# Last stage of an attention and feed-forward kernel: inverse norms from a logarithm, an exponential and a Newton step per half tile, applied one tile later, with the rotation joined in place in six buffers

## The chip, the core and the metric

The kernel runs on one core of a Trainium2 chip. The metric is the device time of one execution in microseconds (us). The time before is the median of three runs.

## The reference

The program is a stack of four parts on `x` of shape (2, 512, 128): a cross attention, a mixture of attention experts, a second cross attention, and a six-layer local-attention transformer. The change lies in the last part alone, called stage D here. Cut to what matters, each of its six layers computes

```
x = attn_layer(shift_tokens(x), Wqkv[i], q_scale[i], k_scale[i], Wo[i]) + x
x = ffn_layer(shift_tokens(x), ln_g[i], ln_b[i], W1[i], b1[i], W2[i], b2[i]) + x

attn_layer:
  q, k, v = split(x @ Wqkv)                  # 16 heads of 64
  q = q / max(norm(q), 1e-12) * q_scale      # norm per token and head
  k = k / max(norm(k), 1e-12) * k_scale
  q = q * cos * scale + rotate_half(q) * sin * scale
  k = k * cos / scale + rotate_half(k) * sin / scale
  softmax over a window of 32 + 32 keys, times v, times Wo
```

The inverse norm is one number per token and head, so it commutes with the rotation: the kernel rotates the unnormalised q and k and multiplies by the inverse norm afterwards.

## The kernel before, in words

Stage D (`stage_d`) starts at about 1220 us of a 2410 us span. The 1024 tokens are 8 tiles of 128 (four per batch element). A layer's projection of a tile is cut in four chunks of 512 columns: chunks 0 and 1 are q, 2 and 3 are k, each of 8 heads. Chunk number `k = 4n + c` is chunk c of tile n.

One chunk passes through five engines. TensorE (PE) multiplies (L1256) into the PSUM bank `PM[:, 0]`; ScalarE (ACT) copies it to `RAW` (L1414) and squares it to `SQ` (L1423); VectorE (DVE) multiplies `RAW` by the tables into `R1` and, halves swapped, into `R2` (L1492 to L1494), sums the squares per head (L1496) and floors the sum (L1498); GpSimd (POOL) adds `R1 + R2` into `QR` (L1211), raises the eight floored sums to the power -0.5 (L1213) and multiplies `QR` by them (L1216). One tile later PE turns (transposes) the four 128-column blocks of `QR` into `PX` (L144, called from `proj`), and ACT copies them to `QT` or `KT` (L1419). Behind the turn, in the same chunk, PE makes v (L1269) in bank `PM[:, 1]`.

PE's part of a chunk is written so: first matmul L1256 of chunk k, then

```
wait(roped, k - 4)
wait(turned_out, k - 5)
for i in range(4):
    mm = turn(m, pe, PX[:, i * 128:(i + 1) * 128], QR[:, k % 4, i * 128:(i + 1) * 128])
```

and then the v matmuls. `roped` is what POOL's multiplication L1216 counts. Every engine runs its instructions strictly in its own order.

That order comes from a list written out by hand, `layer_order()`: for each step k of 0 to 12 it names pieces with a number, and each engine carries out what it has to do for a piece. Steps 9 to 12 of a layer are interleaved with steps 0 to 3 of the next (`BODY`, sorted by step and number), so one pass of the loop has steps 0 to 8. In step k, PE does: `score` of tile k-2 (L1281), `pturn` of tile k-3 (probabilities turned), `proj` chunk 0, chunk 1, `mix` (probabilities times v, L1302), chunk 2, `oturn`, chunk 3, and `out` (L1322). DVE does, in this order: the score's mask, maximum and subtraction (L1503, L1506, L1508), chunk 0, chunk 1, the weighting of the mixed values (L1519), chunk 2, the sum of the probabilities (L1511), chunk 3, and the addition of `out` (L1523). The feed-forward part has pieces `f1a`, `f1b`, `f2`, `f3`, `f4`. For one batch element they fall in steps 7 and 8, for the other in steps 2 and 3. In `f1b`, between chunks 1 and 2 (behind `mix`), DVE takes the variance (L1529 to L1537), POOL raises it to -0.5 (L1220) and DVE scales (L1540). In `f3`, ACT's Gelu (L1453) needs a table load, and so does the next Exp (L1431).

`R1`, `R2`, `RAW` and `SQ` have two buffers each, `QR` four. DVE therefore waits for `roped` of chunk k-2 before it writes `R1` of chunk k.

Of the kernel before, what the change touches and what calls it, by code (L numbers as in the profile page):

```python
# [13 lines left out]
ALU = mybir.AluOpType  # L14
# [1015 lines left out]
def layer_order():  # L1030
# [7 lines left out]
    for k in range(NT + 5):  # L1038
# [53 lines left out]
def stage_d(nc, shared, d, V, out):  # L1092
    with ExitStack() as ctx:
# [9 lines left out]
        HALF = m.sb("DHALF", [128, 8])  # L1103
        XS = m.sb("DXS", [128, B, W + S])
        RAW, SQ = m.sb("DRAW", [128, 2, 512]), m.sb("DSQ", [128, 2, 512])
        R1, R2, QR = m.sb("DR1", [128, 2, 512]), m.sb("DR2", [128, 2, 512]), m.sb("DQR", [128, 4, 512])
        SS, RN = m.sb("DSS", [128, 2, 8]), m.sb("DRN", [128, 2, 8])
# [15 lines left out]
        def ev(name, per, credit=0):  # L1123
            return Event(m.sem("d_" + name), per, credit)
# [27 lines left out]
        with nc.Block() as block:  # L1152
# [78 lines left out]
            def _(pe):  # L1231
                for e in (turned, oturned):
                    pe.sem_inc(e.sem, e.credit)
                pe.wait_ge(padded, 3)
                def piece(layer, name, n):
# [9 lines left out]
                    def proj(n, c):  # L1245
# [138 lines left out]
            def _(act):  # L1384
                s = nc.scalar
                norm.scalar(act)
                for e in (turned_out, ot_out):
                    act.sem_inc(e.sem, e.credit)
                act.wait_ge(padded, 3)
                def piece(layer, name, n):  # L1390
# [15 lines left out]
                    if name == "shift":  # L1406
                        shift(n)
                    elif name == "proj":
# [39 lines left out]
                    elif name == "f3":  # L1448
# [4 lines left out]
                        s.activation(GE[0:k, n % 2, :], PM[0:k, 0, :], ACT.Gelu, bias=COLS[0:k, 5 + n % 3:6 + n % 3]).then_inc(pm0.drained, 1)  # L1453

# [9 lines left out]
            def _(dve):  # L1464
# [7 lines left out]
                def piece(layer, name, n):  # L1472
# [9 lines left out]
                    if name == "proj" and n[0] < NT:  # L1482
# [3 lines left out]
                        r1, r2 = (r[:, k % 2, :].rearrange("p (h e) -> p h e", h=8) for r in (R1, R2))  # L1486
# [4 lines left out]
                        wait(roped, k - 2)  # L1491
# [183 lines left out]
```

## Time and profile before

| | |
|---|---|
| median of 3 runs | 2403.64 us (2400.76 to 2413.32) |
| the profiled execution's own time | 2412.02 us |
| its span in the profile | 2410.2 us |
| PE busy | 1975.7 us (82%) |
| DVE busy | 1761.9 us (73%) |
| ACT busy | 1441.7 us (60%) |
| POOL busy | 1028.0 us (43%) |
| mean granted TensorE clock | 0.921 of full speed |

The profile is of one execution. Busy times are averages over four stages with different limits. Stage D is a loop of six layers, and an inner layer repeats every 194.6 us (from 1783.1 to 1977.7 us, for example), so its parts are read in one such stretch. TensorE's clock has two levels, 2.4 GHz (shown as 1.00) and 1.2 GHz (0.50).

### The profile page before, as it was taken

What the parts mean: (1) busy time and instruction counts of PE and PEld (TensorE: products, weight loads), DVE (VectorE), ACT (ScalarE), POOL (GpSimd) and SP (SyncE); (2) the same over time, 40 slices, a digit from 0 to 9 for tenths busy, and PEclk for the clock granted to TensorE, in tenths of its full rate; (3) what the DMA queues carried; (4) which work ended last, traced back from release to release, by engine and by line L of the source; (5) the groups of instructions that cost most, each with busy time, mean ns of one, the idle gap of its engine ahead of it and who ended that gap; (6) DMA issues with size and microseconds to landing.
All of it is one profiled execution on the core that took longest, in us unless ns stands there. A gap on an engine that the chain in (4) does not pass through costs nothing. (4 is left out here: it accounts for less than half of the span.)

```text
span 2410.2 us, 52856 instructions
## 1 busy us (share of the span) xinstructions
PE 1975.7 (82%) x18992; PEld 932.5 (39%) x18992; DVE 1761.9 (73%) x3039; ACT 1441.7 (60%) x2138; POOL 1028.0 (43%) x1009
## 2 busy tenths in 40 slices
PE   6745888888888888888568888988987988988886
PEld 3531222222222222222225554554554554554454
DVE  4745677767777777777459977967968868887893
ACT  4312566656666666666456676765856757666663
POOL 0011111111111111110268866856858758777680
PEclk8856899989999999999778999999999999999998
DMA  1012222222222232321010000000000000000000
GB/s 33 1 41 59 48 61 53 59 45 62 48 61 49 54 61 55 62 55 29 3 58 2 31 10 12 30 3 21 2 31 10 12 31 10 12 31 11 12 2 10
DMA packets 52106, 77.07 MB, mean 32 GB/s; under 512 B 10899, under 2 KB 45749, under 8 KB 48053
## 3 DMA queue, kind: packets, MB, share of 16 engines
q1 hardware_dynamic: 49781, 73.27, 13.4%
q8 instruction: 137, 2.24, 0.4%
q10 hardware_dynamic: 2112, 0.94, 0.2%
q14 instruction: 76, 0.62, 0.1%
HBM read 47.70 MB, written 25.69 MB: 30 GB/s over the span
## 5 line engine op out<-in xcount | busy, mean ns | idle before, releaser
L899 DVE TENSOR_REDUCE ENM<-PM 128x1 f32<-128x512 f32 x1024 | 657.7, 685 | 254.2 <-PE PM L722 246.0
L819 ACT ACTIVATE EPT<-PA 128x1024 f32<-128x1024 f32 x512 | 512.6, 1021 | 221.6 <-PE PA L734 138.1
L722 PE MATMUL PM<-EKX,EQX 48*128 48x512 bf16 x1024 | 355.4, 400 | 104.5 <-DVE ENM L899 84.0
L1213 POOL TENSOR_TENSOR DRN<-DRN,DHALF 128x8 f32<-128x8 f32 x192 | 364.4, 1898 | 7.4
L1211 POOL TENSOR_TENSOR DQR<-DR 128x512 f32<-128x512 f32 x192 | 244.3, 1273 | 248.1 <-DVE DR L1494 245.3
L642 POOL CAST ENMP<-ENM 128x16 bf16<-128x16 f32 x64 | 12.6, 196 | 784.9 <-DVE ENM L899 784.9
L744 PE MATMUL PV<-EPT,EVP 128*32 128x512 f32 x2048 | 284.8, 629 | 0.9 <-ACT EPT L819 0.7
L734 PE MATMUL PA<-EQX,EKX 51*128 51x512 bf16 x1024 | 254.1, 395 | 27.6 <-DMA EQX<-EROWS 14.5
L722 PEld LDWEIGHTS PM<-EKX,EQX 48*128 48x128 bf16 x1024 | 85.8, 95 | 482.1 <-DVE ENM L899 393.3
L1256 PE MATMUL PM<-DWQKV,DXS 128*128 128x512 f32 x384 | 216.4, 646 | 39.3 <-ACT XNT L1453 23.2
L1492 DVE TENSOR_TENSOR DR<-DRAW,DTAB 128x512 f32<-128x512 f32 x192 | 193.8, 1009 | 61.6 <-POOL DQR L1216 28.2
L1427 ACT ACTIVATE DV<-PM 64x512 f32<-64x512 f32 x384 | 225.4, 587 | 11.1 <-PE PM L1269 8.9
L1269 PE MATMUL PM<-DWQKV,DXS 128*64 128x512 f32 x768 | 213.5, 632 | 18.1 <-ACT DV L1427 14.7
L1216 POOL TENSOR_TENSOR DQR<-DQR,DRN 128x512 f32<-128x512 f32 x192 | 209.1, 1089 | 27.5
L1414 ACT ACTIVATE DRAW<-PM 128x512 f32<-128x512 f32 x192 | 114.9, 598 | 106.7 <-PE PM L1256 77.1
L144 PEld LDWEIGHTS PX<-IDENT,DQR 128*128 128x128 f32 x768 | 98.1, 145 | 101.7 <-issue 96.5
L144 PE MATMUL PA<-IDENT,DP 128*128 128x128 f32 x768 | 116.5, 295 | 17.4 <-DVE DP L1519 17.2
L1496 DVE TENSOR_REDUCE DSS<-DSQ 128x8 f32<-128x512 f32 x192 | 129.3, 673 | 0.0
L1322 PE MATMUL PV<-DWO,DOT 128*128 128x128 f32 x768 | 106.7, 297 | 22.2 <-DVE XN L1540 20.7
L1423 ACT ACTIVATE DSQ<-DRAW 128x512 f32<-128x512 f32 x192 | 121.7, 634 | 0.8
L1322 PEld LDWEIGHTS PV<-DWO,DOT 128*128 128x128 f32 x768 | 98.1, 207 | 56.2 <-issue 32.8
L144 PE MATMUL PX<-IDENT,DQR 128*128 128x128 f32 x768 | 118.7, 278 | 0.6 <-POOL DQR L1216 0.6
(204 smaller groups left out, 2932.7 us busy)
## 6 DMA issues: line engine op xcount, KB each, us to landing
e_park<-EPARTS SPq DMA_DIRECT2D x64, 192.0 KB, 2.9
EQX<-e_park SPq DMA_DIRECT2D x32, 384.0 KB, 5.7
EKX<-e_park SPq DMA_DIRECT2D x32, 384.0 KB, 9.3
DWQKV<-in_WqkvR SPq DMA_DIRECT2D x6, 1536.0 KB, 6.2
e_park<-EPARTS SPq DMA_DIRECT2D x64, 128.0 KB, 2.7
e_park<-EPARTS SPq DMA_DIRECT2D x64, 64.0 KB, 2.2
EQX<-EROWS ACTq DMA_DIRECT2D x256, 3.0 KB
DWO<-in_WoR SPq DMA_DIRECT2D x6, 512.0 KB, 4.3
```

The lines of the kernel that those rows point to most:

```text
L144: return pe.matmul(out, lhsT=in_, rhs=m.IDENT[0:k, 0:k], is_transpose=True, start=True, stop=True)
L722: pe.matmul(PM[:, r, :], lhsT=QX[64 * r:64 * r + KQ, b, hp, t * 128:(t + 1) * 128], rhs=KX[64 * r:64 * r + KQ, b, hp, :], start=True, stop ...
L734: mm = pe.matmul(PA[:, 2 * pair + r, :], lhsT=KX[64 * r:64 * r + KS, b, hp, kt * 128:(kt + 1) * 128], rhs=QX[64 * r:64 * r + KS, b, hp, :] ...
L744: mm = pe.matmul(PV[32 * j:32 * j + 32, :], lhsT=VP[:, g // HG, kt, 4 * (g % HG) + j, :], rhs=PT[:, kt, j * S:(j + 1) * S], start=kt == 0, ...
L819: s_.activation(PT[:, kt, pair * 2 * S:(pair + 1) * 2 * S], PA[:, 2 * pair:2 * pair + 2, :].rearrange("p a b -> p (a b)"), ACT.Exp, scale= ...
L899: v.tensor_reduce(NM[:, g % 2, t, j, 0:1], PM[:, r, :], AX.X, ALU.max, negate=True).then_inc(maxed, 1)
L1211: g.tensor_tensor(qr, r1, r2, ALU.add).then_inc(joined.sem, 1)
L1213: g.tensor_tensor(rn, rn, HALF[:, 0:8], ALU.pow).then_inc(rooted.sem, 1)
L1216: g.tensor_tensor(qr.rearrange("p (h e) -> p h e", h=8), qr.rearrange("p (h e) -> p h e", h=8), bc(rn, 2, [128, 8, DL]), ALU.mult).then_in ...
L1256: pe.matmul(PM[:, 0, :], lhsT=XS[:, b, W + t * 128:W + (t + 1) * 128], rhs=WQKV[:, c * 512:(c + 1) * 512], start=True, stop=True).then_inc ...
L1269: mm = pe.matmul(PM[64 * par:64 * par + 64, 1, :], lhsT=keys, rhs=wv[:, par], start=True, stop=True)
L1427: ins = s.activation(V[r, n % 4, c, :, par, :], PM[r, 1, :].rearrange("p (h e) -> p h e", h=HP), ACT.Copy)
```

## The change

All of it is in stage D. The power on POOL is replaced. DVE's sums of squares go to one tile-wide buffer `SS`, and a new piece `floor` (DVE, L1536 of the changed kernel) floors a half tile (16 sums) at once and multiplies it by -0.5. A new piece `guess` (ACT, L1435 and L1438) takes the logarithm and the exponential of minus half of it. A new piece `root` (POOL, L1223 to L1229) makes one Newton step in four operations of 128x16. The join is done in place: DVE writes its first product straight to `QR`, which now has six buffers, and POOL adds `R2` to it (L1240). The multiplication by the inverse norm (L1236) of chunk k-4 is issued in chunk k, ahead of the join of chunk k. DVE's wait for `roped` of chunk k-2 is replaced by waits for `turned` of chunk k-6 and `joined` of chunk k-2. ACT is told to load one table set for both functions at the stage's start and behind the last Gelu of each `f3` group. The power for the layer norm (`f1b`) stays on POOL.

```diff
@@ layer_order @@
+            if c == 2 and k < NT:
+                order.append((k, at - 2, "floor", 2 * k))
+            if c == 2 and 1 <= k <= NT:
+                order.append((k, at - 2, "root", 2 * k - 1))
             if k <= NT:
                 order.append((k, at, "proj", (k, c)))
+            if c == 0 and 1 <= k <= NT:
+                order.append((k, at + 2, "guess", 2 * k - 1))
+            if c == 2 and k < NT:
+                order.append((k, at + 2, "guess", 2 * k))
...
+        if k < NT:
+            order.append((k, 47, "floor", 2 * k + 1))
+            order.append((k, 47, "root", 2 * k))
@@ gpsimd @@
-                    elif name == "proj" and n[0] < NT:
+                    elif name == "root":
+                        half = slice(16 * (n % 2), 16 * (n % 2) + 16)
+                        ss, rn = SS[:, n // 2 % 2, half], RN[:, n // 2 % 2, half]
+                        pool.wait_ge(guessed.sem, guessed.at(layer, n))
+                        g.tensor_tensor(NEWT[:, :], rn, rn, ALU.mult).then_inc(newton.sem, 1)
...
+                        g.tensor_tensor(rn, rn, NEWT[:, :], ALU.mult).then_inc(rooted.sem, 1)
+                    elif name == "proj":
                         k = 4 * n[0] + n[1]
-                        r1, r2, rn = (x[:, k % 2, :] for x in (R1, R2, RN))
-                        qr = QR[:, k % 4, :]
-                        pool.wait_ge(rotated.sem, rotated.at(layer, k))
-                        pool.wait_ge(turned.sem, turned.at(layer, k - 4))
-                        g.tensor_tensor(qr, r1, r2, ALU.add).then_inc(joined.sem, 1)
-                        pool.wait_ge(floored.sem, floored.at(layer, k))
-                        g.tensor_tensor(rn, rn, HALF[:, 0:8], ALU.pow).then_inc(rooted.sem, 1)
...
+                        if n[0]:
+                            qr, rn = QR[:, (k - 4) % 6, :], RN[:, (n[0] - 1) % 2, 8 * n[1]:8 * n[1] + 8]
+                            pool.wait_ge(joined.sem, joined.at(layer, k - 4))
+                            pool.wait_ge(rooted.sem, rooted.at(layer, 2 * (n[0] - 1) + n[1] // 2))
+                            g.tensor_tensor(qr.rearrange("p (h e) -> p h e", h=8), qr.rearrange("p (h e) -> p h e", h=8),
+                                            bc(rn, 2, [128, 8, DL]), ALU.mult).then_inc(roped.sem, 1)
+                        if n[0] < NT:
+                            pool.wait_ge(rotated.sem, rotated.at(layer, k))
+                            g.tensor_tensor(QR[:, k % 6, :], QR[:, k % 6, :], R2[:, k % 2, :], ALU.add).then_inc(joined.sem, 1)
@@ scalar @@
+                s.preload_act_table_set("natural_log_exp_and_others")
...
+                    elif name == "guess":
+                        half = slice(16 * (n % 2), 16 * (n % 2) + 16)
+                        wait(floored, n)
+                        s.activation(LOGS[:, :], SS[:, n // 2 % 2, half], ACT.Ln, scale=-2.0).then_inc(logged.sem, 1)
+                        wait(logged, n)
+                        wait(roped, 2 * (n - 4) + 1)
+                        s.activation(RN[:, n // 2 % 2, half], LOGS[:, :], ACT.Exp, scale=-0.5).then_inc(guessed.sem, 1)
...
+                        if n % 3 == 2:
+                            s.preload_act_table_set("natural_log_exp_and_others")
@@ vector @@
-                        wait(roped, k - 2)
+                        wait(turned, k - 6 if k >= 6 else -1)
                         v.tensor_tensor(r1, x, bc(tab[:, 0], 1, [128, 8, DL]), ALU.mult).then_inc(step, 1)
+                        wait(joined, k - 2)
...
-                        v.tensor_reduce(SS[:, k % 2, :], SQ[:, k % 2, :].rearrange("p (h e) -> p h e", h=8), AX.X, ALU.add).then_inc(summed.sem, 1)
-                        wait(summed, k)
-                        v.tensor_scalar(RN[:, k % 2, :], SS[:, k % 2, :], 1e-24, None, ALU.max).then_inc(floored.sem, 1)
+                        if c % 2 == 0:
+                            wait(rooted, 2 * (n[0] - 2) + c // 2)
+                        v.tensor_reduce(SS[:, n[0] % 2, 8 * c:8 * c + 8], SQ[:, k % 2, :].rearrange("p (h e) -> p h e", h=8), AX.X, ALU.add).then_inc(summed.sem, 1)
+                    elif name == "floor":
+                        half = slice(16 * (n % 2), 16 * (n % 2) + 16)
+                        wait(summed, 2 * n + 1)
+                        v.tensor_scalar(SS[:, n // 2 % 2, half], SS[:, n // 2 % 2, half], 1e-24, -0.5, ALU.max, ALU.mult).then_inc(floored.sem, 1)
```

POOL's order before, one chunk of any step (`DQR`, `DRN` and the like are the buffers `QR` and `RN` of the text):

```order
L1209 REGISTER_ALU
L1211 TENSOR_TENSOR DQR<-DR1,DR2 128x512 [waits d_turned,d_rotated]
L1213 TENSOR_TENSOR DRN<-DRN,DHALF 128x8 [waits d_floored]
L1216 TENSOR_TENSOR DQR<-DQR,DRN 128x512 [waits d_rooted,d_joined]
```

POOL's order in the changed kernel, chunks 0 and 1 of a step with the half-tile step that stands between them and chunk 2:

```order
L1235 REGISTER_ALU [waits d_joined]
L1236 TENSOR_TENSOR DQR<-DQR,DRN 128x512 [waits d_rooted]
L1239 REGISTER_ALU
L1240 TENSOR_TENSOR DQR<-DQR,DR2 128x512 [waits d_rotated]
L1236 TENSOR_TENSOR DQR<-DQR,DRN 128x512 [waits d_rooted,d_joined]
L1239 REGISTER_ALU
L1240 TENSOR_TENSOR DQR<-DQR,DR2 128x512 [waits d_rotated]
L1223 TENSOR_TENSOR DNEWT<-DRN 128x16 [waits d_guessed]
```

The first L1236 belongs to chunk k-4 and the L1240 behind it to chunk k; the second L1236 stands behind that L1240, which waits for DVE's rotation.

ACT's order in step 3 of the changed kernel, from `f3`'s first Gelu (L1484) to the second; L1458 is v, L1470 `oturn`:

```order
L1484 ACT_TABLE_LOAD
L1484 ACTIVATE XNT<-PM,DCOLS 128x512
...
L1458 ACTIVATE DV<-PM 64x8x64 x2
L1416 REGISTER_ALU
L1435 ACT_TABLE_LOAD
L1435 ACTIVATE DLOGS<-DSS 128x16
L1438 ACT_TABLE_LOAD
L1438 ACTIVATE DRN<-DLOGS 128x16
L1470 ACTIVATE DOT<-PA 128x512 x2
L1481 REGISTER_ALU
L1419 REGISTER_ALU
L1484 ACT_TABLE_LOAD
```

Before, the first of these loads was there and the other three were not.

## Rows read from the trace of the kernel before

**Rows 1.** The page: busy us, share of the span, instructions of each engine.

```profile
PE 1975.7 (82%) x18992; PEld 932.5 (39%) x18992; DVE 1761.9 (73%) x3039; ACT 1441.7 (60%) x2138; POOL 1028.0 (43%) x1009
```

**Rows 2.** Windows: us, busy PE, PEld, DVE, ACT, POOL, clock, DMA, GB/s.

```profile
1783.10:1977.70 194.60, 167.97 (x2220) 101.95 (x2222) 155.10 (x260) 127.23 (x220) 140.06 (x102) 0.95 0.06 17
...
1914.30:1933.30 19.00, 17.46 (x267) 10.62 (x266) 18.24 (x29) 14.03 (x26) 17.57 (x13) 1.00 0.01 2
...
1856.30:1865.20 8.90, 8.22 (x21) 4.18 (x22) 7.37 (x15) 4.09 (x7) 8.61 (x7) 0.51 0.01 2
...
1950.40:1954.00 3.60, 3.60 (x20) 3.48 (x22) 3.35 (x6) 0.00 (x0) 1.84 (x2) 0.53 0.67 279
```

**Rows 3.** Timeline of POOL, steps 5 and 6: start, us, instruction, idle before.

```profile
1901.82 1.28 POOL L1211 TENSOR_TENSOR DQR<-DR 128x512 f32<-128x512 f32 x1 [2.43 <-DVE DR L1494]
1903.21 2.04 POOL L1213 TENSOR_TENSOR DRN<-DRN,DHALF 128x8 f32<-128x8 f32 x1
1905.39 1.04 POOL L1216 TENSOR_TENSOR DQR<-DQR,DRN 128x512 f32<-128x512 f32 x1
...
1918.39 1.49 POOL L1216 TENSOR_TENSOR DQR<-DQR,DRN 128x512 f32<-128x512 f32 x1
```

**Rows 4.** Groups by line: busy us, mean ns, idle before.

```profile
L1213 POOL TENSOR_TENSOR DRN<-DRN,DHALF 128x8 f32<-128x8 f32 x192 | 364.4, 1898 | 7.4
...
L1498 DVE TENSOR_SCALAR DRN<-DSS 128x8 f32<-128x8 f32 x192 | 78.9, 411 | 6.6
...
L644 POOL TENSOR_TENSOR ENM<-ENM,ENMP 128x16 f32<-128x16 f32 x64 | 14.3, 223 | 5.1
...
L1453 ACT ACT_TABLE_LOAD x12 | 15.4, 1283 | 0.3 <-ACT XN L1445 0.2
...
L127 ACT ACTIVATE STD<-STD 128x8 f32<-128x8 f32 x4 | 0.8, 208 | 12.0 <-DVE STD L117 12.0
```

**Rows 5.** Timeline of PE, step 5, and the `out` of step 7.

```profile
1895.66 1.09 PE L144 MATMUL PA<-IDENT,DP 128*128 128x128 f32 x8
...
1898.99 1.12 PE L1256 MATMUL PM<-DWQKV,DXS 128*128 128x512 f32 x2
1899.95 0.60 PE L144 MATMUL PX<-IDENT,DQR 128*128 128x128 f32 x4
...
1913.41 1.09 PE L144 MATMUL PA<-IDENT,DP 128*128 128x128 f32 x8
...
1950.37 3.67 PE L1322 MATMUL PV<-DWO,DOT 128*128 128x128 f32 x16 [3.44 <-DVE XN L1540]
```

**Rows 6.** Timeline of DVE, steps 5 and 6.

```profile
1895.86 1.23 DVE L1503 TENSOR_TENSOR DP<-PA,DMASK 128x1024 f32<-128x1024 f32 x1 [0.28 <-PE PA L1281]
...
1901.66 0.67 DVE L1496 TENSOR_REDUCE DSS<-DSQ 128x8 f32<-128x512 f32 x1
...
1903.64 0.42 DVE L1493 TENSOR_TENSOR DR<-DRAW,DTAB 128x256 f32<-128x256 f32 x1
...
1914.63 1.23 DVE L1503 TENSOR_TENSOR DP<-PA,DMASK 128x1024 f32<-128x1024 f32 x1 [0.24 <-DVE Y L1523]
...
1918.29 0.68 DVE L1492 TENSOR_TENSOR DR<-DRAW,DTAB 128x512 f32<-128x512 f32 x1
```

**Rows 7.** Timeline of DVE and POOL in `f1b`, step 2.

```profile
1833.53 0.89 DVE L1529 BATCH_NORM_STATS2 ST<-PV 128x6 f32<-128x128 f32 x4
...
1834.99 1.10 DVE L1537 TENSOR_SCALAR STD<-MV 128x4 f32<-128x4 f32 x1
...
1838.81 1.01 POOL L1220 TENSOR_TENSOR RSTD<-STD,DHALF 128x4 f32<-128x4 f32 x1
...
1839.85 1.36 DVE L1540 TENSOR_SCALAR XN<-PV,MV,RSTD 128x128 f32<-128x128 f32 x4 [3.76 <-POOL RSTD L1220]
```

**Rows 8.** Timeline, step 8: PE's score and DVE's first operation on it.

```profile
1953.97 1.49 PE L1281 MATMUL PA<-DKT,DQT 64*32 64x64 f32 x128
...
1958.69 1.22 DVE L1503 TENSOR_TENSOR DP<-PA,DMASK 128x1024 f32<-128x1024 f32 x1 [0.25 <-DVE Y L1523]
```

More of the change, by code:

```diff
@@ L1102, in stage_d @@
         MASK = m.sb("DMASK", [128, 2, DL])
-        HALF = m.sb("DHALF", [128, 8])
+        HALF = m.sb("DHALF", [128, TB])
         XS = m.sb("DXS", [128, B, W + S])
         RAW, SQ = m.sb("DRAW", [128, 2, 512]), m.sb("DSQ", [128, 2, 512])
-        R1, R2, QR = m.sb("DR1", [128, 2, 512]), m.sb("DR2", [128, 2, 512]), m.sb("DQR", [128, 4, 512])
-        SS, RN = m.sb("DSS", [128, 2, 8]), m.sb("DRN", [128, 2, 8])
+        QR, R2 = m.sb("DQR", [128, 6, 512]), m.sb("DR2", [128, 2, 512])
+        SS, RN = m.sb("DSS", [128, 2, 32]), m.sb("DRN", [128, 2, 32])
+        LOGS, NEWT, THREE = (m.sb(x, [128, 16]) for x in ("DLOGS", "DNEWT", "DTHREE"))
         QT = m.sb("DQT", [128, 2, HP, 128])
@@ L1136, in stage_d @@
         summed, rotated = ev("summed", 4 * NT, 2), ev("rotated", 4 * NT, 2)
-        floored = ev("floored", 4 * NT)
-        joined, rooted = ev("joined", 4 * NT), ev("rooted", 4 * NT)
-        roped = ev("roped", 4 * NT, 2)
+        floored, logged, guessed = ev("floored", 2 * NT), ev("logged", 2 * NT), ev("guessed", 2 * NT)
+        joined, rooted, newton = ev("joined", 4 * NT, 2), ev("rooted", 2 * NT, 4), ev("newton", 6 * NT)
+        roped = ev("roped", 4 * NT, 8)
         turned, turned_out = ev("turned", 4 * NT, 4), ev("turned_out", 4 * NT, 1)
@@ L1191, in _ @@
                 g.memset(HALF[:, :], -0.5).then_inc(padded, 1)
+                g.memset(THREE[:, :], 1.5).then_inc(padded, 1)
                 g.memset(XS[:, :, :], 0.0).then_inc(padded, 1)
                 g.memset(KT[:, :, :, 0:W], 0.0).then_inc(padded, 1)
-                pool.wait_ge(padded, 3)
+                pool.wait_ge(padded, 4)
                 pool.wait_ge(const, 32)
-                pool.sem_inc(roped.sem, roped.credit)
+                for e in (roped, joined, rooted):
+                    pool.sem_inc(e.sem, e.credit)
                 def piece(layer, name, n):
@@ L1233, in _ @@
                     pe.sem_inc(e.sem, e.credit)
-                pe.wait_ge(padded, 3)
+                pe.wait_ge(padded, 4)
                 def piece(layer, name, n):
@@ L1261, in proj @@
                             for i in range(4):
-                                mm = turn(m, pe, PX[:, i * 128:(i + 1) * 128], QR[:, k % 4, i * 128:(i + 1) * 128])
+                                mm = turn(m, pe, PX[:, i * 128:(i + 1) * 128], QR[:, (k - 4) % 6, i * 128:(i + 1) * 128])
                             mm.then_inc(turned.sem, 1)
@@ L1485, in piece @@
                         x = RAW[:, k % 2, :].rearrange("p (h e) -> p h e", h=8)
-                        r1, r2 = (r[:, k % 2, :].rearrange("p (h e) -> p h e", h=8) for r in (R1, R2))
+                        r1, r2 = (r.rearrange("p (h e) -> p h e", h=8) for r in (QR[:, k % 6, :], R2[:, k % 2, :]))
                         tab = TAB[:, 2 * (c // 2):2 * (c // 2) + 2, t, :]
```

11 lines of the change are left out of this document (6 added, 5 removed).

## The prediction

> **What bounds the kernel now.** I read the page's busy shares first: PE leads with 82%, POOL is lowest with 43% [rows 1]. These are averages over four stages, so I went on to windows of stage D, the only stage touched. An inner layer lasts 194.6 us, with PE busy 168.0, DVE 155.1 and POOL 140.1 [rows 2]. PE alone can't give back more than 194.6 - 168.0 = 26.6 us a layer. Then the chain of waits through stage D and the timelines of its engines: for some stretches POOL leads. Its three operations of a chunk, one behind the other, take 1905.39 + 1.04 - 1901.82 = 4.6 us, of which the power is 2.04 [rows 3]; over the stage the power costs 364.4 us on POOL [rows 4]. In other stretches PE runs without a gap and POOL has idle time (2.43 us ahead of 1901.82 in rows 3). The reader is to see two facts: POOL's power is on the path in part of each layer only, and PE never waits for POOL's multiplication to turn `QR`, because it was made four chunks before.
>
> **What is removed.** 192 powers of 1.9 us on POOL [rows 4], so POOL ceases to lead. 192 floors of 0.41 us on DVE (78.9 us) become 96 for 16 columns each; at the same price a piece DVE saves some 39 us, beside PE's work. New on ACT: 96 pairs of small operations, nearest row 0.21 us each [rows 4], 40 us in all, in the gaps of an engine that is busy 127 of 194.6 us [rows 2]: taken at nothing, except in step 3 (below). New on POOL: 96 times four operations of 128x16. The nearest row is 0.22 us each [rows 4]; each waits for the one before, and the step from the end of L1211 to the start of L1213, 0.11 us in rows 3, is a lower bound for that. I take 1.5 us per half tile (upper bound: four times the power's 1.9, if small operations cost by their count, which the 0.22 row speaks against).
>
> **What is moved, and what it does to PE.** This is the term that decides. PE's turn in chunk k needs the multiplication of chunk k-4. It now stands on POOL behind the join of chunk k-1, and that join waits for DVE's rotation of chunk k-1. Before, PE could be a chunk or two ahead of DVE at no cost. Now PE cannot pass chunk k's turn until DVE has rotated chunk k-1 and POOL has joined it and multiplied.
>
> Chunk 1 of a step is the worst place, since DVE starts each step with the score. Step 5 is worked out from its rows. PE finishes the score at 1895.66 and, unhindered, reaches chunk 1's turn at 1899.95: 4.3 us later [rows 5]. DVE starts the score's mask 0.2 us after PE's end and has rotated chunk 0 when L1496 starts. Step 6 shows the score uncontended: 1918.29 - 1914.63 = 3.7 us [rows 6]. A rotation is 1.3 us (three operations of 0.68, 0.42 and 0.42, which overlap by a little). Then 0.15 us to POOL, 1.28 for the join, 1.04 for the multiplication [rows 3], 0.1 to PE. Sum: 0.2 + 3.7 + 1.3 + 0.15 + 1.28 + 1.04 + 0.1 = 7.8 us. DVE's L1492 of chunk 1 is by then waiting, and a multiplication that met one took 1.49 instead of 1.04 [rows 3]: 8.2 us. **Term A: a stall of 8.2 - 4.3 = 3.9 us** (3.5 without the contention) in steps 2, 4, 5, 6 and 7: 19.5 us a layer. Even the rotation of the old trace, done at 1901.66 [rows 6], is already 1.7 us too late for PE.
>
> **Term B.** In chunk 3 only `oturn` lies between. From the end of chunk 2's L1256 PE needs the turn (0.6), v and `oturn` (an estimate: each as long as L1256) and chunk 3's L1256, 1899.95 - 1898.99 = 0.96 [rows 5]: 3.4 us. ACT's copy (an estimate, as long as a turn with its signal: 0.7), the rotation (1.4), join and multiplication (2.5 with signals) take 4.6. The difference is 1.2 us in steps 1, 4, 5 and 6, so 4.8.
>
> **Term C, the clock.** When PE idled 3.44 us ahead of 1950.37, the granted clock was at its lower level, 1.2 GHz, for nearly all of the next 3.6 us (mean 0.53) [rows 2, 5]: 3.6 x 0.47 = 1.7 us lost at most. Elsewhere it stayed low for 8.9 us (0.51) [rows 2], which costs up to 4.4. Stall A is longer than 3.44 us, so I expect the fall in each such step, and everything behind it up to the next score is on the path. I take the smaller loss, 1.6 each: 8.0.
>
> Steady steps come out thus: 4.3 + 3.9 + 13.1 (from chunk 1's turn to the end of the next score, 1913.41 - 1899.95 less 0.4 of idle time [rows 5]) + 1.2 + 1.6 = 24 us, where step 5 took 1913.41 - 1895.66 = 17.75.
>
> **Term D.** In steps 2 and 7 the half-tile step and chunk 2's multiplication are queued on POOL behind the layer norm's power, which waits for DVE's variance. From L1529 the chain is 1.5 (statistics), 1.1, 1.0 (power) [rows 7], then 1.5 and 1.0 to the turn, 5 us of stall in each step beyond term A's place. In step 7 PE's wait of 3.44 and the slow `out` (1.6) go away. In step 2 the power started 2.7 us after its input was there (1834.99 + 1.10) [rows 7], since POOL was busy, and I count 2 of that as won. Net: 10 - 5 - 2 = +3.0.
>
> **Term E.** In step 3 the logarithm and the exponential stand between two Gelus of `f3`. The listing has a load for each of them and one for the next Gelu: 3 x 1.28 + 0.4 = 4.3 us [rows 4], of which about 1.0 fills a gap: +3.3.
>
> The Trainium skill, ScalarE: Activation LUTs, section Table sets, says that ln and then exp take a single load because one set holds both. By that rule term E would be 2.0 and the total 8 us lower. The listing shows two loads there, and listing and row decide.
>
> **Term F.** Steps 0 and 1: DVE is free of POOL (-1), but chunk 0 of step 1 now waits for the half-tile step and a multiplication (1.5 + 1.0, less 0.5 of slack): +1.0. **Gains G:** DVE ran 3.3 us behind PE's score in step 8 (1958.69 against 1955.4) [rows 8], and PE will no longer have run ahead: -3.3. PE's gaps in step 6, 19.0 - 17.46 us [rows 2]: -1.5. Step 3, where PE waits for DVE's score in the same way: another -1.5.
>
> Sum for a layer: 19.5 + 4.8 + 8.0 + 3.0 + 3.3 + 1.0 - 6.3 = **33.3 us**. Six layers make 200. The first layer starts with eight chunks that POOL paces at its 4.6 us; four without a turn and four with one gain about 10 us: +190. On the profiled execution's 2412.0 us that is 2602; it is 8.4 us above the median of the runs, 2403.6, and against that I forecast 2594.
>
> **A rule that speaks for the change.** During the power that began at 1903.21 and took 2.04 us, DVE's L1493 ran at 1903.64 in 0.42 us, its undisturbed time [rows 3, 6]. So the power doesn't hold up DVE, and I gave its removal nothing there. The Trainium skill, SBUF — State Buffer, section on the port layout, says that a GpSimd instruction holds the port it shares with VectorE for its whole length against an instruction with two SBUF inputs. By that rule removing the powers would free DVE too, and every term that ends in a rotation would shrink. The row speaks against it here.
>
> **The rivals.**
> 1. *The same coupling, but cheap.* The multiplication wins against L1492 (stall 3.5), the clock holds, and the steps with `f1b` cost nothing. A layer gets 33.3 - 2.0 - 8.0 - 3.0 = 20.3 us longer: 2404 + 122 - 10 = 2516. For it: the fall behind 3.44 us is the only one that I have at about this length, and a stall that is cut in two by a signal might not do it. Against it: 3.5 is still over 3.44.
> 2. *Faster.* The end is set by POOL's power, and PE's waits for the turn only replace its later waits for DVE. With POOL's power gone, up to 26.6 us a layer are to be had; half of that over six layers gives 2404 - 80 = 2324. For it: POOL leads the chain wherever it has no gap, and DVE loses two waits. Against it: steps 4 and 5 have no PE gap that could be exchanged. It decides if the new stalls sum up to less than about 13 us a layer, 2 us a step.
> 3. *No change:* gains and stalls cancel, 2404.
> 4. *Dearer:* each stall keeps the clock low as long as after 1856.3, so that term C is 20 us instead of 8: 2594 + 72 = 2666.
>
> **How the numbers follow.** Forecast 0.54, rival 1 0.24, rival 2 0.11, rival 3 0.04, rival 4 0.07. The range 2475 to 2655 holds the first two and half of what lies between, about 8 in 10. Over 0.5% (what a measurement of this kernel can tell from no change) slower: 0.85, within it: 0.04, faster: 0.11.
>
> **What would show it.** Right: among PE's waits, `PX` released by POOL's L1236, some 3 to 5 us once a step at chunk 1 and about 1 us at chunk 3; a steady step near 24 us; a mean clock under 0.95 in a layer; POOL idle for more of the layer than before; three more table loads a layer. Wrong: PE turns without waiting for POOL, or steps of 17 to 18 us as before. If the stalls are there and the clock stays at 1.00 behind them, term C fails and rival 1 holds.

## The result and the profile after

The changed kernel took 2600.45 us, the median of four runs (2589.68 to 2616.16), against 2404.20 us for the kernel before. The ratio is 1.079, with a 95% interval of 1.076 to 1.083. Forecast was 2594, in a range of 2475 to 2655. The profiled execution took 2601.13 us over a span of 2599.3.

The page's busy shares, the same columns as [rows 1]:

```profile
PE 2032.2 (78%) x18992; PEld 932.9 (36%) x18992; DVE 1660.8 (64%) x2943; ACT 1516.0 (58%) x2346; POOL 746.0 (29%) x1202
```

No engine has much more to do. POOL lost 282 us of work and DVE 101; ACT gained 74, and PE 57 with the same 18992 matmuls, which is a lower clock (0.905 of full speed in the mean, 0.921 before). Nothing here explains 196 us; the order of waiting does. The waits of the second half of the span (us in total, times, longest):

```profile
POOL DQR L1240 <- DVE DR L1528: 670.8, 190, 21.6
PE PX L144 <- POOL DQR L1236: 201.8, 96, 4.6
```

PE stood 201.8 us before the turn of `QR`, released by the multiplication L1236, in 96 places, two for each tile and layer in the mean. POOL stood 670.8 us before its join. Before the change PE's turns waited 0.6 us for the multiplication in the whole execution (the group of these turns, columns as in [rows 4]):

```profile
L144 PE MATMUL PX<-IDENT,DQR 128*128 128x128 f32 x768 | 118.7, 278 | 0.6 <-POOL DQR L1216 0.6
```

One inner layer from turn of the probabilities to the same turn (columns as in [rows 2]), then its steps 3, 4, 5, 6 and 7, and a stretch within step 5:

```profile
1879.61:2104.69 225.08, 176.11 (x2218) 101.92 (x2218) 138.38 (x245) 139.90 (x255) 92.86 (x134) 0.92 0.05 14
...
1942.03:1980.87 38.84, 29.62 (x316) 17.16 (x309) 19.43 (x32) 24.17 (x38) 11.80 (x17) 0.91 0.01 2
1980.87:2003.68 22.81, 19.08 (x266) 10.84 (x265) 14.98 (x26) 16.19 (x31) 10.51 (x16) 0.93 0.10 28
2003.68:2027.91 24.23, 19.20 (x271) 10.99 (x265) 16.18 (x26) 15.01 (x29) 11.59 (x17) 0.93 0.01 2
2027.91:2051.48 23.57, 18.86 (x269) 10.84 (x265) 16.20 (x26) 15.00 (x29) 10.97 (x16) 0.93 0.01 2
2051.48:2079.73 28.25, 21.37 (x279) 12.46 (x273) 18.08 (x39) 16.27 (x31) 10.91 (x16) 0.88 0.08 24
...
2011.60:2017.00 5.40, 5.36 (x73) 3.15 (x74) 2.14 (x5) 3.35 (x5) 3.14 (x6) 0.68 0.01 3
```

The layer of 194.6 us [rows 2] became 225.1, and the chip-wide difference is made of that: 22.9 us in the first layer, 30.5 to 33.4 in each of the four between, 33.8 in the last, from the same turn in each layer of both traces, plus 5.1 us by which stage D began later. PE's timeline in step 5 answers to [rows 5]:

```profile
2003.68 1.09 PE L144 MATMUL PA<-IDENT,DP 128*128 128x128 f32 x8
...
2007.01 1.12 PE L1279 MATMUL PM<-DWQKV,DXS 128*128 128x512 f32 x2
2011.64 0.96 PE L144 MATMUL PX<-IDENT,DQR 128*128 128x128 f32 x4 [3.51 <-POOL DQR L1236]
2012.53 1.98 PE L1292 MATMUL PM<-DWQKV,DXS 128*64 128x512 f32 x4
2014.44 2.33 PE L1325 MATMUL PA<-DV,DPT 128*32 128x128 f32 x64
...
2022.33 0.65 PE L144 MATMUL PX<-IDENT,DQR 128*128 128x128 f32 x4 [1.18 <-POOL DQR L1236]
```

The turn of chunk 1, which stood right behind L1256 in [rows 5], now waits 3.51 us, and chunk 3's waits 1.18. Behind the first wait L1292 takes 1.98 us instead of 1.08: PE runs at the 1.2 GHz level. The window above gives 0.68 of full speed for these 5.4 us. POOL, over the same wait (answers to [rows 3]):

```profile
2002.65 0.22 POOL L1229 TENSOR_TENSOR DRN<-DRN,DNEWT 128x16 f32<-128x16 f32 x1
...
2008.88 1.26 POOL L1240 TENSOR_TENSOR DQR<-DQR,DR 128x512 f32<-128x512 f32 x1 [4.88 <-DVE DR L1528]
2010.10 1.49 POOL L1236 TENSOR_TENSOR DQR<-DQR,DRN 128x512 f32<-128x512 f32 x1
2012.28 1.27 POOL L1240 TENSOR_TENSOR DQR<-DQR,DR 128x512 f32<-128x512 f32 x1 [0.70 <-DVE DR L1528]
2013.51 0.21 POOL L1223 TENSOR_TENSOR DNEWT<-DRN 128x16 f32<-128x16 f32 x1
...
2014.70 1.04 POOL L1236 TENSOR_TENSOR DQR<-DQR,DRN 128x512 f32<-128x512 f32 x1
```

POOL idles 4.88 us until DVE has rotated chunk 0 of the tile, joins it, and only then multiplies chunk 1 of the tile before (1.49 us, with DVE's L1525 and L1527 beside it). The inputs of that multiplication were complete at 2002.65 + 0.22 = 2002.87 us, when the Newton step ended; its join lay four chunks back. It began 7.2 us later; chunk 0's own multiplication took 1.04 of these, and its place behind the join the rest. From L1223 to the next L1236 the Newton step takes 14.70 - 13.51 = 1.2 us for a half tile.

### The profile page after: what moved, and what is told of

Same layout as the page of the kernel before. It is cut to its first block, busy times and chain, and to the rows that moved or that the text cites. A ratio compares the mean times of both kernels' runs of the same rounds, so it can differ in the third digit from the quotient of the medians.

```text
span 2599.3 us, 53427 instructions
## 1 busy us (share of the span) xinstructions
PE 2032.2 (78%) x18992; PEld 932.9 (36%) x18992; DVE 1660.8 (64%) x2943; ACT 1516.0 (58%) x2346; POOL 746.0 (29%) x1202
## 4 chain that ended last, share of the span: by engine, by line
issue 32%; POOL 16%; PE 2%; ACT 1%; DVE 1%; POOLq 1%; DMA 0%; SPq 0%; DVEq 0%; ACTq 0%
POOL DQR L1236 7%; POOL DQR L1240 5%; POOL DNEWT L1227 1%; POOL DRN L1229 1%; POOL DNEWT L1225 1%; POOL DNEWT L1223 1%; PE PM L1292 1%; PE PM L1279 1%; POOL DTAB L1217 1%; DMA DWQKV<-in_WqkvR 0%; ACT DRAW L1445 0%; PE PX L144 0%; PE PA L1325 0%; DVE DQR L1525 0%; ACT DV L1458 0%
## 5 line engine op out<-in xcount | busy, mean ns | idle before, releaser
L1240 POOL TENSOR_TENSOR DQR<-DQR,DR 128x512 f32<-128x512 f32 x192 | 243.8, 1270 | 670.8 <-DVE DR L1528 670.8
L144 PE MATMUL PX<-IDENT,DQR 128*128 128x128 f32 x768 | 131.4, 297 | 204.3 <-POOL DQR L1236 201.8
L1525 DVE TENSOR_TENSOR DQR<-DRAW,DTAB 128x512 f32<-128x512 f32 x192 | 151.4, 788 | 157.5 <-ACT DRAW L1445 148.0
L1458 ACT ACTIVATE DV<-PM 64x512 f32<-64x512 f32 x384 | 226.2, 589 | 32.2 <-PE PM L1292 29.9
L1292 PE MATMUL PM<-DWQKV,DXS 128*64 128x512 f32 x768 | 241.4, 711 | 3.4 <-ACT DV L1458 3.4
L1279 PE MATMUL PM<-DWQKV,DXS 128*128 128x512 f32 x384 | 222.0, 662 | 14.2 <-ACT XNT L1484 6.5
L1236 POOL TENSOR_TENSOR DQR<-DQR,DRN 128x512 f32<-128x512 f32 x192 | 204.6, 1068 | 8.9
L1325 PEld LDWEIGHTS PA<-DV,DPT 128*32 128x32 f32 x3072 | 97.3, 126 | 57.3 <-issue 54.3
L1325 PE MATMUL PA<-DV,DPT 128*32 128x128 f32 x3072 | 113.8, 309 | 2.8 <-ACT DPT L1466 2.0
L144 PE MATMUL PA<-IDENT,DP 128*128 128x128 f32 x768 | 110.7, 290 | 0.8 <-DVE DP L1557 0.6
L1450 ACT ACTIVATE DQT<-PX 128x512 f32<-128x512 f32 x96 | 57.1, 595 | 90.3 <-PE PX L144 90.2
```

The source lines that it names most:

```text
L144: return pe.matmul(out, lhsT=in_, rhs=m.IDENT[0:k, 0:k], is_transpose=True, start=True, stop=True)
L1240: g.tensor_tensor(QR[:, k % 6, :], QR[:, k % 6, :], R2[:, k % 2, :], ALU.add).then_inc(joined.sem, 1)
L1279: pe.matmul(PM[:, 0, :], lhsT=XS[:, b, W + t * 128:W + (t + 1) * 128], rhs=WQKV[:, c * 512:(c + 1) * 512], start=True, stop=True).then_inc ...
L1292: mm = pe.matmul(PM[64 * par:64 * par + 64, 1, :], lhsT=keys, rhs=wv[:, par], start=True, stop=True)
L1325: mm = pe.matmul(PA[32 * w:32 * w + 32, 2 + hp // 4, hp % 4 * 128:(hp % 4 + 1) * 128], lhsT=PT[:, hp, w * W:(w + 1) * W], rhs=V[:, n % 4, ...
L1458: ins = s.activation(V[r, n % 4, c, :, par, :], PM[r, 1, :].rearrange("p (h e) -> p h e", h=HP), ACT.Copy)
```

## The experiments

Each kernel was timed beside the kernel before on the same chip. They came in four groups (changed; e1 to e4; e5 to e8; e9 to e12), in which the kernel before had medians of 2404.2, 2407.4, 2411.4 and 2404.5 us, so a difference of kernels from two groups is uncertain by some us. The last column is the mean of the four inner layers in the profiled execution.

| kernel | median us | ratio, 95% interval | layer |
|---|---|---|---|
| before | 2404.2 | 1 | 194.4 |
| changed | 2600.5 | 1.079 (1.076 to 1.083) | 226.2 |
| e1_early | 2372.5 | 0.984 (0.978 to 0.990) | 189.4 |
| e2_power | 2651.3 | 1.102 (1.095 to 1.109) | 234.0 |
| e3_before_inplace | 2411.1 | 1.002 (0.999 to 1.004) | 194.1 |
| e4_filled | 2565.6 | 1.067 (1.060 to 1.075) | 222.0 |
| e5_guess_late | 2548.9 | 1.058 (1.055 to 1.061) | 219.0 |
| e6_early_late | 2342.9 | 0.972 (0.969 to 0.975) | 182.7 |
| e7_early_power | 2411.7 | 1.001 (0.999 to 1.003) | 193.7 |
| e8_later | 3503.0 | 1.454 (1.446 to 1.461) | 378.4 |
| e9_after_again | 2597.6 | 1.081 (1.077 to 1.084) | 228.2 |
| e10_filled_again | 2563.7 | 1.067 (1.063 to 1.070) | 220.5 |
| e11_late_filled | 2533.2 | 1.054 (1.051 to 1.057) | 217.0 |
| e12_guess_late_again | 2552.6 | 1.061 (1.058 to 1.065) | 219.2 |

**The multiplication one chunk earlier.** Theory: the time lies in the place of the multiplication, a turn of chunk k waiting for the join of chunk k-1. In chunk k POOL now multiplies for chunk k+1's turn, so that PE waits for what was joined two chunks ago:

```
-                        if n[0]:
-                            qr, rn = QR[:, (k - 4) % 6, :], RN[:, (n[0] - 1) % 2, 8 * n[1]:8 * n[1] + 8]
-                            pool.wait_ge(joined.sem, joined.at(layer, k - 4))
+                        if 0 <= k - 3 < 4 * NT:
+                            t, c = divmod(k - 3, 4)
+                            qr, rn = QR[:, (k - 3) % 6, :], RN[:, t % 2, 8 * c:8 * c + 8]
+                            pool.wait_ge(joined.sem, joined.at(layer, k - 3))
```

`root` moves with it, from ahead of chunks 0 and 2 to ahead of chunks 3 and 1.

> The changed kernel, with POOL's multiplication of a chunk issued one chunk earlier (chunk k-3 in chunk k, ahead of the join of chunk k), and the half-tile Newton step ahead of chunks 1 and 3. PE's turn then hangs on the join of two chunks before, not of the last one. Theory (the turn's wait for POOL is the loss): terms A, B, C and most of D go, the table loads of step 3 (some 20 us in all) stay, and the gains remain: 2350 to 2420 us, and PX released by POOL in PE's waits falls from 202 us to under 40. Rival (the new arithmetic, its table loads and small operations are the loss): 2560 to 2600.

Measured: 2372.5 us, 228 below the changed kernel and 1.6% below the kernel before, on the same arithmetic. PE's wait for the multiplication fell from 201.8 to 35.8 us. One chunk of distance, for the multiplication together with the Newton step that it needs, is the whole loss, and hides a gain.

**The old power in the new place.** Logarithm, exponential and Newton step go; POOL takes the power for 16 columns at a time:

```
-                        g.tensor_tensor(NEWT[:, :], rn, rn, ALU.mult).then_inc(newton.sem, 1)
...
-                        g.tensor_tensor(rn, rn, NEWT[:, :], ALU.mult).then_inc(rooted.sem, 1)
+                        g.tensor_tensor(rn, ss, HALF[:, :], ALU.pow).then_inc(rooted.sem, 1)
```

> The changed kernel with the old arithmetic: POOL raises a half tile's 16 floored sums to the power -0.5 where the Newton step stood; no logarithm, exponential, Newton step or table request on ACT. The multiplication stays one tile late. Theory: the placing alone makes the loss, so 2560 to 2610 (some 20 us less for the table loads, a little back for a power of about 2 to 3.5 us in place of the Newton step's 1.5). Rival (arithmetic is the loss): 2400 to 2440.

Measured: 2651.3 us, beyond the changed kernel by 51. The waits and the power's group:

```profile
PE PX L144 <- POOL DQR L1227: 262.2, 100, 7.4
```

```profile
L1220 POOL TENSOR_TENSOR DRN<-DSS,DHALF 128x16 f32<-128x16 f32 x96 | 280.8, 2925 | 0.0
```

The sign was right, the size too small. The power of 16 columns takes 2.9 us, and at chunks 0 and 2 it stands between the join and the multiplication that PE waits for, where Newton's chain takes 1.2. So the new arithmetic helps even here; with e1_early beside it, the loss is order.

**The old order with the buffers joined in place.** The kernel before, with `R1` gone and `QR` in six buffers:

```
-R1, R2, QR = m.sb("DR1", [128, 2, 512]), m.sb("DR2", [128, 2, 512]), m.sb("DQR", [128, 4, 512])
+QR, R2 = m.sb("DQR", [128, 6, 512]), m.sb("DR2", [128, 2, 512])
...
-                        g.tensor_tensor(qr, r1, r2, ALU.add).then_inc(joined.sem, 1)
+                        g.tensor_tensor(qr, qr, r2, ALU.add).then_inc(joined.sem, 1)
```

> The kernel before, with only the join in place in six buffers (DVE writes its first product to QR, waits for turned of chunk k-6 and joined of chunk k-2); the power and the multiplication stay behind each chunk's own join. Theory: POOL's pace and PE's turns stay as they were, so within 0.5% of before, 2392 to 2416. Rival (joining in place or the new waits of DVE cost something): over 2430.

Measured: ratio 1.002 with 1 inside the interval. The join in place, in the old order, costs and gives nothing.

**Keeping PE busy in the wait.** Sixteen turns of the identity into `PX`, which the real turn overwrites, ahead of chunk 1's wait in steps 2 to 7. It adds matmuls and leaves the data alone:

```
+                            wait(turned_out, k - 5)
+                            if c == 1 and 2 <= n < NT:
+                                pe.sem_inc(pe_passed, 1)
+                                for i in range(FILL):
+                                    turn(m, pe, PX[:, i % 4 * 128:(i % 4 + 1) * 128], m.IDENT[:, :])
                             wait(roped, k - 4)
-                            wait(turned_out, k - 5)
```

The wait for `turned_out` moves ahead of the one for `roped`; the real turn stands behind both as before.

> The changed kernel with 16 turns of the identity into PX (some 2.3 us of PE's time, overwritten by the real turn) ahead of the wait for the multiplication in chunk 1 of steps 2 to 7, so that PE is busy in most of the stall. Theory (term C, the fall of the clock behind the stall costs 1.6 us each time): stalls stay where they are but the clock behind them stays at its higher level, 8 us a layer less, 2540 to 2570. Rival (the clock's fall is hidden or isn't due to the stall): 2590 to 2610.

Measured: 2565.6 us. But this trace had entered stage D 14.8 us sooner than the changed kernel's, in stages that are the same in both, and the layers were shorter by 4.2 us only. So it was repeated with the changed kernel beside it:

> The changed kernel itself, so that the three that follow have it beside them on the same chip. Expected: 2600, ratio 1.079, as in its own comparison. In the first look the changed kernel's profiled execution entered stage D 14.8 us later than the filled one's (first L1279 at 1231.68 against the first L1280 at 1216.91), in stages that are the same in both, so part of the 35 us between them may belong to no edit. If so, this run comes out nearer to 2585.

> The same kernel as e4_filled. What term C (the clock's fall behind the stall) is worth: from this kernel's own layers, turn of the probabilities to the same turn a layer on, 223 us against 225.4, I expect 2.5 to 5 us a layer, so 15 to 30 us below e9_after_again. If the first comparison held, 35 below. If the clock is worth nothing, within 5 us of it.

Measured: 2597.6 and 2563.7 us, 33.9 apart, so 5.7 us a layer; the profiled layers differ by 7.7. The medians repeat. The profiled executions leave a doubt that no run settles: in all three kernels with the filling turns stage D begins at 1211.6 to 1216.9 us, in every other trace here at 1218.3 to 1231.7, though the stages ahead of it are the same in all. So some us of the 34 may lie ahead of stage D; within it the profiled executions are 35.3 us apart in this pair and 25.6 in the first. The same place in step 5 of the filled kernel, PE's timeline:

```profile
1976.37 1.91 PE L145 MATMUL PX<-IDENT 128*128 128x128 f32 x16
1980.05 0.66 PE L145 MATMUL PX<-IDENT,DQR 128*128 128x128 f32 x4 [1.77 <-POOL DQR L1237]
1980.63 1.08 PE L1297 MATMUL PM<-DWQKV,DXS 128*64 128x512 f32 x4
1981.64 1.96 PE L1330 MATMUL PA<-DV,DPT 128*32 128x128 f32 x64
```

The turn still comes at the same distance from the step's start (7.97 us; 7.96 in the changed kernel), but an idle time of 1.77 us has taken the place of 3.51, and the turn, the v matmuls and the mix behind it take 0.66, 1.08 and 1.96 us instead of 0.96, 1.98 and 2.33. Since the turn came no sooner, these 1.6 us are the clock alone.

**The guess of step 3 behind the last Gelu.** The logarithm and the exponential of the fourth tile's first half move from between two Gelus to behind them:

```
-            if c == 2 and k < NT:
-                order.append((k, at + 2, "guess", 2 * k))
+            if c == (3 if k == 3 else 2) and k < NT:
+                order.append((k, 46.5 if k == 3 else at + 2, "guess", 2 * k))
```

> The changed kernel with the logarithm and exponential of tile 3's first half moved behind the last Gelu of f3 in step 3 (number 46.5 in place of 32), so that three of the layer's table loads go. Theory (term E): 3.3 us a layer in the five layers that have this step, 2580 to 2590; if the trace's idle time of 4.8 us ahead of the last gate matmul of step 3 is all theirs, with the slow clock behind it, up to 6 us a layer, 2568. Rival (loads are hidden by the stalls on the turn): 2595 to 2605.

> The same kernel as e5_guess_late, 2549 there, now beside the changed kernel on the same chip. Expected: 35 to 50 us below e9_after_again; term E would then be 6 to 10 us in each of the five layers that it meets, where 3.3 was forecast.

Measured: 2548.9 us where the changed kernel took 2600.5 in its own comparison, and 2552.6 beside 2597.6: 45 to 52 us, or 9 to 10 in each of the five layers that have the three loads. That is nearly three times term E. ACT in step 3 of the changed kernel, then what PE does meanwhile there, then PE in the same place of e12_guess_late_again:

```profile
1961.92 1.28 ACT L1435 ACT_TABLE_LOAD   x1
1963.21 0.21 ACT L1435 ACTIVATE DLOGS<-DSS 128x16 f32<-128x16 f32 x1
1963.45 1.28 ACT L1438 ACT_TABLE_LOAD   x1
...
1966.08 1.28 ACT L1484 ACT_TABLE_LOAD   x1
```

```profile
1949.60 0.66 PE L144 MATMUL PX<-IDENT,DQR 128*128 128x128 f32 x4 [2.73 <-POOL DQR L1236]
...
1957.98 1.12 PE L1279 MATMUL PM<-DWQKV,DXS 128*128 128x512 f32 x2 [1.29 <-ACT XNT L1484]
...
1968.12 2.00 PE L1386 MATMUL PM<-XN,DW 128*85 128x512 f32 x2 [4.82 <-ACT XNT L1484]
1969.91 1.51 PE L1388 MATMUL PM<-XN,DW 128*85 128x512 f32 x2
...
1988.08 1.12 PE L144 MATMUL PX<-IDENT,DQR 128*128 128x128 f32 x4 [2.01 <-POOL DQR L1236]
1989.13 1.98 PE L1292 MATMUL PM<-DWQKV,DXS 128*64 128x512 f32 x4
```

```profile
1936.24 1.09 PE L1386 MATMUL PM<-XN,DW 128*85 128x512 f32 x2 [0.34 <-ACT XNT L1484]
1937.17 1.02 PE L1388 MATMUL PM<-XN,DW 128*85 128x512 f32 x2
...
1955.02 0.66 PE L144 MATMUL PX<-IDENT,DQR 128*128 128x128 f32 x4 [2.00 <-POOL DQR L1236]
1955.61 1.08 PE L1292 MATMUL PM<-DWQKV,DXS 128*64 128x512 f32 x4
```

The gate matmul waited 4.82 us instead of 0.34 and then ran at the lower level: 4.5 + 1.4 us. And in step 4 the same stall (2.01 and 2.00) is followed by the low clock in one kernel and by full speed in the other: 1.4 us more. The windows of steps 3 and 4 of e12_guess_late_again say the same, 33.19 us against 38.84, and 21.30 against 22.81. Below them are the same two steps of e9_after_again, the changed kernel once more:

```profile
1914.63:1947.82 33.19, 28.45 (x316) 16.57 (x310) 19.43 (x32) 20.22 (x35) 11.53 (x17) 0.95 0.01 2
1947.82:1969.12 21.30, 17.80 (x266) 10.23 (x265) 15.33 (x26) 16.23 (x31) 10.24 (x16) 1.00 0.12 30
...
1936.05:1976.51 40.46, 31.24 (x315) 17.71 (x310) 19.42 (x32) 24.32 (x38) 11.61 (x17) 0.87 0.01 2
1976.51:1999.43 22.92, 19.19 (x267) 11.53 (x265) 14.97 (x26) 16.10 (x31) 10.54 (x16) 0.93 0.11 28
```

The layer shown first gives 5.7 + 1.5 = 7.2 us of the 9 to 10. The rest is in layers like the one of e9_after_again, where the low clock of step 3 lasts longer and the step takes 40.5 us. Step 4 takes 22.8 to 22.9 us in all ten layers of the two traces of the changed kernel, and 21.3 in all ten of e5_guess_late and e12_guess_late_again.

**Both mendings together.** Are they two effects or one?

> The late guess of e5_guess_late and the filling turns of e4_filled together. If term E's large price is mainly PE's idle time between two Gelus (4.82 us) and the clock it leaves behind in step 4, and the filling covers stalls in other places, the two gains add: e9_after_again less about 50 less 15 to 30, 2520 to 2535. If both only mend the same low clock, this kernel comes out within 10 us of e12_guess_late_again.

Measured: 2533.2 us, 64.5 below the changed kernel beside it, where the two alone give 45.0 + 33.9 = 78.9. Most of it adds; 14 us don't. Step 4 shows some 8 of them: it takes 22.9 us in the changed kernel, 21.8 with the filling turns, 21.3 with the late guess and 21.8 with both. There the late guess already keeps the clock up, and the filling turns only add 0.5 us. Where the other 6 lie was not followed.

**The early multiplication with the late guess.** In e1_early the gate of step 3 still waited 4.82 us. With the guess behind the last Gelu, ahead of chunk 3 in that step:

```
+            if c == 2 and k < NT and k != 3:
+                order.append((k, at + 2, "guess", 2 * k))
+            if c == 3 and k == 3:
+                order.append((k, at - 3, "guess", 2 * k))
```

> The kernel with the multiplication one chunk earlier, with tile 3's logarithm and exponential behind the last Gelu too. Theory: the same 3.3 to 6 us a layer come off, 2372 less 17 to 30, so 2342 to 2356. Rival (hidden): 2365 to 2380.

Measured: 2342.9 us, 2.8% faster than the kernel before, the fastest here. Its layer and its step 5, windows:

```profile
1752.83:1936.78 183.95, 164.72 (x2218) 98.70 (x2217) 145.13 (x245) 133.82 (x252) 102.18 (x134) 0.96 0.06 18
...
1853.26:1872.39 19.13, 17.47 (x271) 10.55 (x264) 18.03 (x27) 14.76 (x29) 13.42 (x18) 1.00 0.01 2
```

Step 5 is still 1.4 us longer than before the change (17.75): the remaining coupling costs 0.64 us at chunk 3's turn and keeps PE from running ahead. The gain over the kernel before lies in step 3, which takes 30.7 us in this layer instead of 38.3, and in steps 7 and 8, 45.3 instead of 50.5.

**The old power with the early multiplication.** As e1_early, with the power of 16 columns as in e2_power.

> The kernel with the multiplication one chunk earlier, and with the power on POOL for a half tile (2.9 us for 128x16) in place of logarithm, exponential and Newton step. It tells what the arithmetic alone is worth where the turn does not wait. Theory: POOL has 4 x 2.4 + 2 x 2.9 = 15.4 us of work in a step of 17.7, no table loads are added, and the power stands once a half tile ahead of a multiplication: 2380 to 2430, that is slower than with the Newton step by some 10 to 50 us. Rival (the arithmetic is neutral): within 5 us of 2372.

Measured: 2411.7 us, the time of the kernel before. At this place the new arithmetic is worth 2411.7 - 2372.5 = 39 us (40 by the two ratios, since the groups differ), and 69 with the late guess; in the changed kernel's place it was 51.

**The multiplication even later.** The mirror image of e1_early: POOL's join of chunk k goes ahead of its multiplication for chunk k's turn, so that PE waits for the rotation of the very chunk it has just multiplied.

```
-                        <multiplication for chunk k - 4>
                         <join of chunk k>
+                        <multiplication for chunk k - 4>
```

> The changed kernel with the multiplication of chunk k-4 behind the join of chunk k in place of ahead of it, so that PE's turn in chunk k hangs on DVE's rotation of the same chunk: the suspected wait, made longer by one chunk. Theory: all four turns of a step stall, about 5.9 + 3 x 4.6 us where it is now 3.5 + 1.2, so some 13 us more a step and 80 to 100 a layer: 2950 to 3250. Rival (the turn's wait is a symptom of another bound): under 2750.

Measured: 3503.0 us. The direction was right and the size beyond my upper end. A window of one layer and one turn from PE's timeline (1.12 us instead of 0.60):

```profile
1953.13:2332.00 378.87, 222.73 (x2218) 120.98 (x2218) 133.82 (x245) 143.76 (x255) 90.89 (x134) 0.76 0.03 9
```

```profile
2067.48 1.12 PE L144 MATMUL PX<-IDENT,DQR 128*128 128x128 f32 x4 [4.51 <-POOL DQR L1239]
```

Stalls of 4.5 us and more at every chunk were expected; that PE would do nearly all its work between them at the lower clock was not (222.7 us busy for what takes 168.0 in [rows 2]).

## Why the prediction was right

Right in the sign, the mechanism and the sum: 33.3 us a layer against 30.5 in the profiled layer (226.2 - 194.4 = 31.8 over four), and 23.3 against 22.9 in the first layer. That the sum is so near owes something to luck: term A is too large, term E and the gain in step 3 too small, and they cancel. Cut by the same turns in both traces, the terms stand so (measured: after less before, for one layer):

| steps | terms of the forecast | forecast | measured |
|---|---|---|---|
| 0 to 2 | B 1.2, A 3.9, C 1.6, D 3.0, F 1.0 | 10.7 | 11.2 |
| 3 | E 3.3, G -1.5 | 1.8 | 0.6 |
| 4 | A 3.9, B 1.2, C 1.6 | 6.7 | 4.9 |
| 5 | A 3.9, B 1.2, C 1.6 | 6.7 | 6.5 |
| 6 | the same, G -1.5 | 5.2 | 4.6 |
| 7 | A 3.9, C 1.6, D 0 | 5.5 | 5.2 |
| 8 | G -3.3 | -3.3 | -2.5 |
| sum | | 33.3 | 30.5 |

- **Term A** (3.9 us at chunk 1 in steps 2, 4, 5, 6, 7): 3.17, 2.01, 3.51, 3.53 and 2.67 us, 14.9 instead of 19.5. The chain was the forecast's, with the slow multiplication (1.49 us) in it. Step 3 has the same stall, 2.73 us, which I had left out. The reading that PE never waited for the multiplication before was right but for 0.6 us.
- **Term B** (1.2 at chunk 3): 1.18 in steps 4 and 5, 1.19 in step 6, 0.92 in step 1. Right.
- **Term C, the clock** (8.0 a layer): real. PE's busy time for the same matmuls of a layer grew from 168.0 us [rows 2] to 176.1, so by 8.1. The filling turns give 5.7 of it back by the medians; they stand ahead of chunk 1 alone, and the falls behind the stalls of 4.38, 4.82 and 4.21 us in steps 2, 3 and 7 stay. A fall costs 1.4 to 1.6 us in most places, as I took it, but not each stall brings one. Behind the 3.17 us of step 2 the turn and the v matmuls took 0.65 and 1.08, the fast times; behind the 2.67 of step 7 the turn was fast and the v matmuls slow:

```profile
1924.41 0.65 PE L144 MATMUL PX<-IDENT,DQR 128*128 128x128 f32 x4 [3.17 <-POOL DQR L1236]
1925.00 1.08 PE L1292 MATMUL PM<-DWQKV,DXS 128*64 128x512 f32 x4
...
2058.99 0.66 PE L144 MATMUL PX<-IDENT,DQR 128*128 128x128 f32 x4 [2.67 <-POOL DQR L1236]
2059.58 1.96 PE L1292 MATMUL PM<-DWQKV,DXS 128*64 128x512 f32 x4
```

- **Term D** (5 us of stall in steps 2 and 7): 4.38 and 4.21 in the trace. The Newton step took 1.2 us instead of 1.5.
- **Term E** (table loads in step 3, 3.3) was the term worst sized: the runs give 9 to 10. I had counted the loads' 4.3 us less a gap that they fill. They fill none, and what they set off, a stall of 4.82 us with the low clock behind it and a slower step 4, was left out, though term C had just said that stalls do this.
- **Term G in step 3** (-1.5) failed the other way and hid it. Before the change PE waited there for a Gelu, late behind DVE's softmax, and ran at the lower level for some 9 us [rows 2]:

```profile
1849.10 1.21 DVE L1503 TENSOR_TENSOR DP<-PA,DMASK 128x1024 f32<-128x1024 f32 x1
...
1856.32 2.08 PE L1256 MATMUL PM<-DWQKV,DXS 128*128 128x512 f32 x2 [4.64 <-ACT XNT L1453]
```

DVE began the score's mask 9.6 us into the step (1839.51). In the changed kernel it begins it 0.2 us in, since PE no longer runs ahead of it, and the wait is 1.29 instead of 4.64. With the loads out of the way, e12_guess_late_again passes step 3 in 33.2 us (31.7 in another layer) against 38.3 before the change: this gain is at least 5.1 us and not 1.5. So step 3 came out near its forecast by luck, through two errors of opposite sign.

That the step's loads would be two and not one was told from the listing, and the trace has both. The rule of the Trainium skill, ScalarE: Activation LUTs, section Table sets, that one set holds ln and exp, also agrees with a run: in e6_early_late the load at L1490 is followed by the logarithm and the exponential with none between them:

```profile
1825.76 1.28 ACT L1490 ACT_TABLE_LOAD   x1
1827.05 0.22 ACT L1439 ACTIVATE DLOGS<-DSS 128x16 f32<-128x16 f32 x1
1827.30 0.22 ACT L1442 ACTIVATE DRN<-DLOGS 128x16 f32<-128x16 f32 x1
```

The set is there where the program asks for it by name; between the Gelus of the changed kernel nothing did.

That the power doesn't hold up DVE, for which the prediction had one row, is borne out by the whole trace before the change: 123 of DVE's 192 L1493 ran beside the power alone, 0.42 us in the median, as without it. Beside the multiplication L1216 alone it took 1.27.

**The rivals.** Rival 1 (cheap coupling, 2516) needed a clock that holds, and it didn't. Rival 2 (faster, 2324) had named a true gain: with the coupling loosened by one chunk the same arithmetic gives 2372.5, and 2342.9 with the guess moved. It failed on its own condition, stalls under 13 us a layer: they were 201.8 / 6 = 33.6. Rival 4 (the clock stays low, 2666) did not happen here but did in e8_later.

What stays open is why a stall of much the same length is followed by the lower clock in one step and not in another; no run varied that alone. How much of e1_early's 228 us is term A, B or D was not tried apart either: the edit loosens all three, and it moves the Newton step with the multiplication.

## What to carry to other kernels

When work is moved within an engine's queue, ask first what now stands directly ahead of it and what that waits for: the multiplication of chunk 1 had all its inputs 7.2 us before it ran, and the kernel lost 8% because it stood behind a join that waits for another engine's newest chunk. Put work for a consumer at least one piece ahead of its due time, and judge new arithmetic and its new place by separate runs, since better arithmetic (39 us here) can be hidden under a worse place. A small operation that changes ACT's table set between two of a chain that PE waits for should be priced with the stall and the clock behind it, not by its own loads.

## What the runs showed of the hardware

- GpSimd's power costs by its columns: 1.0 us for 128x4, 1.65 to 2.1 for 128x8 (1.9 in the mean), 2.9 for 128x16, while multiplications and additions of 128x16 take 0.22 and start 0.3 us after one another when each waits for the one before.
- The length of a stall alone does not tell whether the granted clock falls behind it. Step 4, with a stall of 2.0 us, has a mean of 0.93 in the changed kernel and of 1.00 in e12_guess_late_again, where the stall of 4.82 us in step 3 before it is gone. Within the changed kernel 3.17 us in step 2 is followed by full speed and 2.01 in step 4 by the lower level. With 4.5 us of idle time at every chunk the mean stayed at 0.76 over a whole layer.
- Idle TensorE time filled with useless turns gave 34 us back (2597.6 to 2563.7), though the awaited turn itself came no sooner after the start of the step (7.97 and 7.96 us in step 5).
